# Graph attention layers: the combine of node slots laid out on 128 partitions instead of 8

## What is computed

```
def _gat(x, src, dst, W, a_src, a_dst, b, concat, n):
    H, C = a_src.shape
    h = (x @ W).reshape(n, H, C)
    s_src = (h * a_src).sum(-1)
    s_dst = (h * a_dst).sum(-1)
    e = jax.nn.leaky_relu(s_src[src] + s_dst[dst], NEG_SLOPE)
    m = jax.ops.segment_max(e, dst, num_segments=n)
    ex = jnp.exp(e - m[dst])
    denom = jax.ops.segment_sum(ex, dst, num_segments=n)
    alpha = ex / (denom[dst] + 1e-16)
    out = jax.ops.segment_sum(h[src] * alpha[:, :, None], dst, num_segments=n)
    ...
```

## Time and profile before

| | us |
|---|---|
| median of 3 runs | 9812.12 (9811.8 to 9825.32) |
| profiled execution | 9830.94 |
| its span, first to last instruction | 9829.6 |
| busy PE, DVE, ACT, POOL | 6069.5, 4056.9, 2194.3, 5760.2 |

### The profile page before, as it was taken

The page is one execution under the profiler, slowest core; times in us unless marked ns, Lnnn a source line. Parts: engine busy times, 40 slices in busy tenths (PEclk is TensorE's granted clock), DMA queues, the critical chain, the costliest instruction groups (busy, mean ns, idle before and its releaser), DMA issues. The chain is left out here.

```text
span 9829.6 us, 120366 instructions
## 1 busy us (share of the span) xinstructions
PE 6069.5 (62%) x43869; PEld 5465.9 (56%) x43869; DVE 4056.9 (41%) x8459; ACT 2194.3 (22%) x5754; POOL 5760.2 (59%) x5804
## 2 busy tenths in 40 slices
PE   4666344445566654544457677776899999963333
PEld 3555344444566644444346676663789888943222
DVE  6666343336444453333544444444221222123333
ACT  0000023331344311333223343431110111011111
POOL 7777577775777756777767777774100000017776
PEclk7555577775788866777668888885799999966666
DMA  5665522220344402222135555540678777821111
GB/s 194 211 212 193 43 60 62 63 62 20 109 115 115 115 23 53 63 63 63 31 103 140 140 140 140 140 133 2 241 275 336 285 287 281 332 104 27 27 27 27
DMA packets 429924, 1241.89 MB, mean 126 GB/s; under 512 B 152450, under 2 KB 215427, under 8 KB 385393
## 3 DMA queue, kind: packets, MB, share of 16 engines
q1 hardware_dynamic: 192308, 744.47, 21.6%
q0 software_dynamic: 237024, 489.72, 19.0%
HBM read 1096.42 MB, written 137.35 MB: 126 GB/s over the span
## 5 line engine op out<-in xcount | busy, mean ns | idle before, releaser
L1161 PE MATMUL ps<-pool 128*106 128x128 f32 (+2 forms) x19344 | 2662.2, 308 | 269.0 <-DVE pool L1067 269.0
L1161 PEld LDWEIGHTS ps<-pool 128*106 128x106 f32 (+2 forms) x19344 | 2633.4, 190 | 281.5 <-DVE pool L1067 281.0
L461 POOL DMA_INDIRECT ACC<-t,ACC x416 | 393.5, 946 | 1962.0 <-issue 1962.0
L1119 ACT ACTIVATE ACC<-ps 72x256 f32 (+1 forms) x2418 | 1012.3, 419 | 1996.0 <-PE ps L1161 1779.9
L743 POOL DMA_INDIRECT cnt_d<-pool x806 | 984.2, 1221 | 544.9 <-PE ps L1340 220.5
L1140 PE MATMUL ps<-ident,pool 128*128 128x128 f32 (+1 forms) x204 | 87.4, 429 | 1657.5 <-DVE pool L1025 1657.5
L1140 PEld LDWEIGHTS ps<-ident,pool 128*128 128x128 f32 (+1 forms) x204 | 35.8, 176 | 1696.7 <-issue 1696.7
L480 PE MATMUL ps<-pool 128*65 128x128 f32 (+1 forms) x2392 | 525.0, 406 | 662.0 <-issue 475.5
L1067 DVE TENSOR_TENSOR pool<-pool,ps 128x1024 f32<-128x1024 f32 (+1 forms) x807 | 928.2, 1213 | 0.0
L1186 POOL DMA_INDIRECT pool<-a_h,srcT_s x806 | 779.7, 967 | 245.7 <-issue 242.4
L1186 POOL DMA_INDIRECT pool<-d_h,srcT_s x806 | 775.9, 963 | 245.6 <-issue 234.0
(11 more groups left out here) (261 smaller groups left out, 8064.0 us busy)
## 6 DMA issues: line engine op xcount, KB each, us to landing
ACC<-cnt_d SPq DMA_DIRECT2D x206, 1600.0 KB, 8.4
pool<-cnt_d SPq DMA_DIRECT2D x104, 1600.0 KB, 8.4
cnt_d<-pool SPq DMA_DIRECT2D x31, 3200.0 KB
ACC<-key_d SPq DMA_DIRECT2D x31, 1664.0 KB, 12.4
pool<-seg_d SPq DMA_DIRECT2D x100, 129.0 KB
cnt_d<-pool POOLq DMA_INDIRECT x806
pool<-a_h,srcT_s POOLq DMA_INDIRECT x806
pool<-b_h,srcT_s POOLq DMA_INDIRECT x806
```

Source lines behind the costliest of these rows:

```text
L461: g.indirect_dma_start(out=gb[b][:, k, :], out_offset=None, in_=table, in_offset=bass.IndirectOffsetOnAxis(ap=idx[:, c:c + 1], axis=0)).th ...
L1119: a.activation(win[:, 0:NPL, bass.ds(reg, 128)], pl[0].rearrange("p (i c) -> p i c", c=128), ACT.Copy).then_inc(*(tile_out if last else A) ...
L1161: mm = t.matmul(o, gbr[:, tile % RT, M * i:M * i + M], oh, start=True, stop=True)
```

## The change

The combine runs on 128 partitions: partition 16 h + q holds head h and the segment q of 248 slots. SP brings `m_` and `den` there with two DMAs (`xm`, `xw`) and the shares back with one. The steps `neg` are loaded once, in layer a. Each node-wide maximum or sum is made by a scan forward and a scan back in every segment, whose ends PE turns to a row of 128; a scan on the row in each direction gives the carries, PE turns them back, and both scans run again from the carries. The sum over a node is forward + back - own value, so the mask `lastS` goes, and `conS` is computed from `neg`. A carry may pass a segment only if the whole segment belongs to one node; these flags (`whole`) come from two reductions, and PE turns them to a row too. The slots' node numbers come by DMA, word by word, in place of the 32 products.

```
-        slot_d = dram("slot_d", (3, 4096))
+        slot_d = dram("slot_d", (1, 4352))
+        QS, CS = 16, SW // 16
+        neg = pool[:, 22045:22045 + CS + 1]
+        first_s, row_d = pool[:, 13000:13000 + NS], dram("row_d", (1, SPL))
         def sync_slot_rows(gi):
             if gi == 10:
-                s.dma_start(slot_d[2:3, 0:SPL - 1], frs[:, 1:SPL]) ...
-                s.dma_start(slot_d[1:2, 0:SPL], grs) ...
+                s.dma_start(slot_d[0:1, 0:SPL], grs) ...
+                s.dma_start(row_d, nrow) ...
             elif gi == 18:
-                s.wait_ge(*mark["slot_cont"])
-                s.dma_start(slot_d[0:1, 0:SPL], frs) ...
+                s.wait_ge(*slot_out.now())
+                s.dma_start(relS[:, 0:NS], row_d[0, 0:SW].rearrange("(b p) -> p b", p=128)) ...
+                firsts = row_d[0, 0:SW].rearrange("(b c) -> b c", c=128)[:, 0]
+                s.dma_start(first_s, firsts.partition_broadcast(128)) ...
+                by_seg = slot_d[0, 0:SW].rearrange("(q c) -> q c", q=QS).unsqueeze(0).to_broadcast([8, QS, CS])
+                s.dma_start(neg[:, 0:CS], by_seg) ...
+                ends = slot_d[0, CS:CS + SW].rearrange(...)[:, 0:1].unsqueeze(0).to_broadcast([8, QS, 1])
+                s.dma_start(neg[:, CS:CS + 1], ends) ...
         def vector_slot_map(gi):
-            elif gi == 14:
-                v.wait_ge(slot_out.sem, 32)
-                v.tensor_scalar(frs, frs, -1.0, 1.0, ALU.mult, ALU.add) ...
+            elif gi == 24:
+                v.wait_ge(rel_in.sem, 32)
+                v.tensor_tensor(out=relS[:, 0:NS], in0=relS[:, 0:NS], in1=first_s, op=ALU.subtract) ...
-        def vector_slot_nodes(): ...
-        def tensor_slot_nodes(): ...
             def sync_slots():
-                s.wait_ge(*tile_mm.now())
+                s.wait_ge(*tile_out.now())
                 s.wait_ge(*wready.now())
-                s.wait_ge(*slot_out.now())
-                for j, o in ((1, negS), (0, conS), (2, lastS)):
-                    s.dma_start(o, slot_d[j, 0:o.shape[1]].partition_broadcast(8)) ...
+                s.dma_start(xm, segments(m_)) ...
+                s.dma_start(xw, segments(den)) ...
                 ...
                 s.wait_ge(*mark["shares"])
+                s.dma_start(segments(den), xw).then_inc(*share_out.one())
                 if following is not None: sync_weights(*following)
+            def vector_wholes():
+                v.memset(nsum[:, :], 0.0)
+                v.tensor_scalar(con, neg, 0.0, None, ALU.is_equal)
+                v.tensor_reduce(out=whole[:, 0:1], in_=neg[:, 0:CS], axis=AX, op=ALU.add)
+                v.tensor_reduce(out=whole[:, 1:2], in_=neg[:, 1:CS + 1], axis=AX, op=ALU.add)
+                v.tensor_scalar(whole[:, 2:4], whole[:, 0:2], 0.0, None, ALU.is_equal)
+                ...
+                v.tensor_copy(wrow, ps[7][0:1, 0:512].rearrange("o (k p) -> o k p", k=4))
+            def vector_scans(x, steps, op0, op1, left, right):
+                v.tensor_tensor_scan(out=fl, data0=steps[:, 0:CS], data1=x, initial=left, ...)
+                v.tensor_tensor_scan(out=rv(fr), data0=rv(steps[:, 1:CS + 1]), data1=rv(x), initial=right, ...)
+            def vector_node(k, x, steps, op0, op1, start):
+                vector_scans(x, steps, op0, op1, start, start)
+                v.wait_ge(ends_mm.sem, em0 + k + 1)
+                v.tensor_tensor_scan(out=crow[:, 0, 1:129], data0=wrow[:, 2 * k, :], data1=ps[5][0:1, 0:128], ...)
+                v.tensor_tensor_scan(out=rv(crow[:, 1, 0:128]), ..., data1=rv(ps[5][0:1, 128:256]), ...)
+                v.wait_ge(carry_mm.sem, cm0 + k + 1)
+                v.tensor_copy(cin, ps[6][:, 0:2])
+                vector_scans(x, steps, op0, op1, cin[:, 0:1], cin[:, 1:2])
             def vector_slots():
+                vector_wholes()
+                v.wait_ge(part_in.sem, ps0 + 32)
+                vector_node(0, xm, neg, ALU.add, ALU.max, -BIG)
+                (maximum of fl and fr, xm - fl, exponential by ACT into fac, xw * fac)
+                vector_node(1, xw, con, ALU.mult, ALU.add, 0.0)
+                (fl + fr - xw, + 1e-16, reciprocal, * fac into xw)
+            def tensor_slots():
+                for k in range(4):
+                    mm = t.transpose(ps[7][0:1, 128 * k:128 * k + 128], whole[:, k:k + 1], ident[:, :])
+                for k in range(2):
+                    t.transpose(ps[5][0:1, 0:128], fl[:, CS - 1:CS], ident[:, :])
+                    t.transpose(ps[5][0:1, 128:256], fr[:, 0:1], ident[:, :])
+                    t.transpose(ps[6][:, 0:1], crow[:, 0, 0:128], ident[0:1, 0:1])
+                    t.transpose(ps[6][:, 1:2], crow[:, 1, 1:129], ident[0:1, 0:1])
             def tensor_merge_slots():
-                t.wait_ge(*mark["shares"])
+                t.wait_ge(share_out.sem, sh0 + 16)
```

More of the change, by code:

```diff
@@ L816, in vector_slot_map @@
                 mark["slot_first"] = V.now()
-            elif gi == 14:
-                v.wait_ge(slot_out.sem, 32)
[L819 to L835, removed]
+            elif gi == 24:
+                v.wait_ge(rel_in.sem, 32)
+                v.tensor_tensor(out=relS[:, 0:NS], in0=relS[:, 0:NS], in1=first_s, op=ALU.subtract).then_inc(*V.one())
         PLANES = {16: (72, 2, 64), 32: (100, 3, 64), 64: (106, 5, 96)}
@@ L1250, in sync_slots @@
                 s.wait_ge(*mark["shares"])
+                s.dma_start(segments(den), xw).then_inc(*share_out.one())
                 if following is not None:
                     sync_weights(*following)
+            def vector_wholes():
+                v.memset(nsum[:, :], 0.0).then_inc(*V.one())
+                v.tensor_scalar(con, neg, 0.0, None, ALU.is_equal).then_inc(*V.one())
+                v.tensor_reduce(out=whole[:, 0:1], in_=neg[:, 0:CS], axis=AX, op=ALU.add).then_inc(*V.one())
+                v.tensor_reduce(out=whole[:, 1:2], in_=neg[:, 1:CS + 1], axis=AX, op=ALU.add).then_inc(*V.one())
+                v.wait_ge(*V.now())
+                v.tensor_scalar(whole[:, 2:4], whole[:, 0:2], 0.0, None, ALU.is_equal).then_inc(*V.one())
+                mark["wholes"] = V.now()
+                v.memset(crow[:, 0, 0:1], 0.0).then_inc(*V.one())
+                v.memset(crow[:, 1, 128:129], 0.0).then_inc(*V.one())
+                v.wait_ge(*t2v.next())
+                v.tensor_copy(wrow, ps[7][0:1, 0:512].rearrange("o (k p) -> o k p", k=4)).then_inc(*V.one())
@@ L1254, in vector_slots @@
             def vector_slots():
-                top, tops, wgt, tot = Z[1][MX:MX + 8, 0:SW], Z[2][MX:MX + 8, 0:SW], Z[1][0:8, 0:SW], Z[2][0:8, 0:SW]
+                v.wait_ge(*tile_mm.now())
                 v.wait_ge(*tile_out.now())
[L1257 to L1260, removed]
+                if layer == 0:
+                    v.wait_ge(*neg_in.now())
@@ L1266, in vector_slots @@
                 mark["slot_x"] = V.now()
                 v.wait_ge(*a2v.next())
[L1268 removed]
+                v.tensor_tensor(out=xw, in0=xw, in1=fac, op=ALU.mult).then_inc(*V.one())
                 v.wait_ge(*V.now())
[L1270 to L1271 removed]
+                vector_node(1, xw, con, ALU.mult, ALU.add, 0.0)
@@ L1277, in vector_slots @@
                 v.wait_ge(*V.now())
-                v.tensor_scalar(den, den, 1e-16, None, ALU.add).then_inc(*V.one())
+                v.reciprocal(fl, fl).then_inc(*V.one())
                 v.wait_ge(*V.now())
-                v.reciprocal(den, den).then_inc(*V.one())
-                v.wait_ge(*V.now())
-                v.tensor_tensor(out=den, in0=den, in1=wgt, op=ALU.mult).then_inc(*V.one())
+                v.tensor_tensor(out=xw, in0=fl, in1=fac, op=ALU.mult).then_inc(*V.one())
                 mark["shares"] = V.now()
```

69 lines of the change are left out of this document (47 added, 22 removed).

## The result

The changed kernel takes 9549.58 us (median of 4 runs, 9545.59 to 9550.8), the kernel before beside it 9811.96. The ratio is 0.973, with a 95% interval of 0.9713 to 0.9746: 262.4 us less.

What follows compares the result with a forecast made beforehand. The prediction saw four combines of long DVE instructions on 8 partitions, 365.8 us with PE idle. At 27.3 us each they become 109.2, gaining 256.6, less 5 in layer a's pass: 251.6, so 9560.5 us, range 9535 to 9600.

Steps and rivals of the forecast that it cites:

- Up to the first scan: Each combine, from the last window copy: DVE's row copy done at 6.4 to 6.5 us, fetch landed at 6.9.
- A pass over a node: Scans, transposes, row scans and carries for one node-wide maximum or sum: 5.35 us, two of them per layer, 10.7.
- Between and behind the node passes: Elementwise steps of the combine: 1.9 us between the two passes, 3.4 after them, reciprocal included.
- The way back: One DMA carrying the shares back to 8 partitions: 2.0 + 2.33 = 4.3 us, bounds 2.0 and 9.0.
- The rule of engines: Transfers: a DMA takes the most engines up to 16 dividing both patterns' slowest dimension, here 8; on 16, 5 us less.
- The two rivals on the exchanges: Fetch and way back: 9.0 us each way, 9588 (chance 0.14), or 2.0 us each, 9545 (chance 0.10).
- Single words in group 18: Layer a's pass: loading 2 x 3968 words puts 46.6 us on SP's queue, with the backlog over before its data is wanted.
- The rival of 746 us: Group 18's single words land 16 times slower than the flags, halting layer a's pass 650 us: 10210; chance 0.02.
- The pass of layer a: Gathers landing late beside the single words cost 5 us, once, between bounds of 0 and 30.
- The merge: Scale products behind each combine: left as they are, granted clock still 0.50.
- the rival of the upper clock: Merge at the upper clock since PE rests only 27 us before it: about 9400; chance 0.02.
- POOL: Count scatters in a and c end 101 to 103 us after the last copy, next work at 132: cover 29 us.

Runs made afterwards that it cites:

- the added loads: Changed kernel plus two unused loads of single words in layer a's pass, 4064 to one partition and 3968 to 128: 9548.52 us (one run).
- the edit: Changed kernel with the merge's scale products reading 128 rows (zero weights on the others) instead of 8: 9394.15 us (one run).

## Why the prediction was right

It gave 9560.5 us, measured were 9549.6. Against the gain of 251.6 us there stand 262.4: 7.4 more in the combines and 5 that the pass did not cost, less 1.6 between a profiled execution and medians.

- **Up to the first scan**: 6.9 forecast, 6.6 measured. Both paths were priced rightly, and they end together: the row copy 6.51 to 6.53 us after the last copy (forecast 6.4 to 6.5), the last landing of the fetch at 6.52 to 6.57 (forecast 6.9). So the fetch had no room to spare: scans that wait for both arrays would start no earlier for shorter DVE work. With the DVE work gone and a wait for the maxima alone, the scan started at 4.4 to 4.5, near the 2.0 + 2.33 us of the price taken from the earlier trace rows.
- **A pass over a node**: 5.35 forecast, 4.69 and 4.68 measured. By steps: two scans 1.30, to the row 0.62 (forecast 0.8), on the row 0.77 (0.94), back 0.41 (0.6), copy 0.20, two scans 1.39. The mis-sized terms are the signals and transposes: two of a pair overlap, 0.42 behind 0.37 us takes 0.59 in all, and so do two scans on DVE. They were added end to end. The same holds for the four transposes of flags, 1.0 for 1.5.
- **Between and behind the node passes**: 1.9 and 3.4 forecast, 1.80 and 3.46 measured, the reciprocal 1.70 as forecast.
- **The way back**: 4.3 forecast, 4.27 measured. The rule of engines (8 of 16) was weighed there and held: 8 landings, and 4 each with four heads in a DMA. That the total fits is partly luck. The price was 2.0 us fixed and 2.33 for the rows; the rows took 1.21, and 3.06 lay around them. The two rivals on the exchanges (9.0 and 2.0 us) fall.
- **Single words in group 18**: this step failed, without harm. Forecast was a backlog of 46.6 us, by the price of the earlier trace rows. They landed 6.0 and 8.4 us after issue. The price was taken from loads to one partition; by the added loads the destination makes a factor of 3.7 (17.4 against 4.7 us). Two loads at 17.4 us would be 34.8, so about a quarter of the 47.7 us of the flags stays open. The rival of 746 us falls with it.
- **The pass of layer a**: 5 us forecast, none measured. The 5 were a choice between two bounds, and the reason given for it, idle engines, was wrong; the loads were over too soon to matter. A load of 17.4 us moved one group by 4.3 us and nothing at the end.
- **The merge**: unchanged at a clock of 0.50, as forecast. But the reason offered against the rival of the upper clock was only that it had not risen before. What holds it down, the products on 8 rows, was not seen, and there lay 155 us. The estimate of that rival, about 9400, is near what the edit gave, 9394.15, but by luck: half of its 400 us of PE would have made 9360, and the edit gave 176, of which the passes took back 26.
- **POOL**: forecast was the end of the scatters 101 to 103 us after the last copy of a, measured 110.5 (2339.40 - 2228.87), and its next work at 130.3 for a forecast 132. In time, as said, with 19.8 us to spare instead of 29.

## What to carry to other kernels

Work on few partitions pays for its columns alone: cutting 8 x 3968 into 128 x 248 took four chains of long instructions from 365.8 to 101.8 us in all, although each scan is now done twice and its carries go through PE. The price of such a scheme could be added up to within 7% (27.3 forecast, 25.5 measured) from a place in the same kernel that does it already; transposes and scans that follow one another on an engine overlap, and counting that would have taken 1.3 of the 1.8 us away. When PE is busy without a break and still at the lower clock, look at how many rows its products read, and after every gain look at the engine that had idle time to lose.

## What the runs showed of the hardware beyond that

- Products that read 8 of 128 rows left PE's granted clock at 0.50 (1.2 GHz) over 159 us of 99.9% busy PE. With 128 rows, most of them against zero weights, the granted clock was 0.98, nearly all at the upper level of 2.4 GHz, and the same merge took 85.0 us, behind 25 us of little PE work as behind 90 us of none (85.9).
- A DVE scan with two SBUF operands held up a POOL scatter until it ended: 7.96 us for 0.97. A tensor_scalar with one SBUF operand did so too (2.98 us), a reciprocal with one did not (0.97). Over the kernel the 806 count scatters (L743) took 984.2 us before and 829.1 after, though nothing on POOL was changed.
- Some 4000 single words landed in 17.4 us on one partition and 4.7 us on 128.
- A DMA between 8 rows on one side and 128 partitions on the other ended with 8 landings, two DMAs of 4 rows with 4 each, and the same bytes then took 3.20 us in place of 1.21.
